# Matmuls without a reader between TensorE's ring steps, in the second half of each head of the first attention

## What is computed

```python
q, k = l2norm(q), l2norm(k)
cos = einsum('bhsd,bhtd->bhst', q, k)
g_dist = arccos(clip(cos, -1 + EPS, 1 - EPS))
attn_score = (1.0 + g_dist) ** (-3.2)
n_r, n_c = attn_score.sum(-1), attn_score.sum(-2)
k_tilde = n_r ** -1 * attn_score * n_c ** -1
probs = k_tilde / maximum(k_tilde.sum(-1), 1e-12)
out = einsum('bhst,bhtd->bhsd', probs, v)
```

## Time and profile before

| | |
|---|---|
| median of 3 runs | 3972.32 us (3971.55 to 3972.55) |
| the profiled execution's own time | 3976.55 us |
| its span, first to last instruction | 3974.8 us |
| mean granted clock of TensorE | 0.784 |
| busy: PE, DVE, ACT, POOL | 81%, 75%, 80%, 30% |
| one head of the loop | 133.12 us |

### The profile page before, as it was taken

One profiled execution on the slowest core, in us unless ns is written; L12 is line 12 of the kernel. 1 busy time (PEld: TensorE's weight loads), 2 busy tenths in 40 slices (PEclk: granted clock), 3 DMA queues, 4 the chain that ended last, 5 costly groups with the idle time before them and its releaser, 6 DMA issues. The chain is left out here.

```text
span 3974.8 us, 59836 instructions
## 1 busy us (share of the span) xinstructions
PE 3205.7 (81%) x18880; PEld 1330.2 (33%) x18880; DVE 2999.1 (75%) x4716; ACT 3186.7 (80%) x2690; POOL 1201.9 (30%) x746
## 2 busy tenths in 40 slices
PE   4777787878787878787877675888888888888899
PEld 2311121112111211121111132355555555555547
DVE  6777877887788777877788798888787787788411
ACT  2799989998999899989999665488788787888822
POOL 2201100110011001101100043377677777777700
PEclk8776566556655665666567698799999999999999
DMA  1000000000000000000000126011001100110000
GB/s 39 31 7 7 0 6 6 6 0 6 6 6 0 6 6 6 0 6 6 6 0 10 35 89 188 22 30 36 23 22 38 28 23 23 39 28 22 20 17 11
DMA packets 59566, 85.93 MB, mean 22 GB/s; under 512 B 9808, under 2 KB 45904, under 8 KB 58960
## 3 DMA queue, kind: packets, MB, share of 16 engines
q1 hardware_dynamic: 59344, 83.06, 7.2%
HBM read 52.44 MB, written 30.54 MB: 21 GB/s over the span
## 5 line engine op out<-in xcount | busy, mean ns | idle before, releaser
L1086 POOL TENSOR_TENSOR lo<-pr,hi 128x1024 f16<-128x1024 f32 x384 | 915.6, 2409 | 391.3 <-ACT hi L1212 389.2
L1135 DVE TENSOR_REDUCE mx<-mx_ps 128x1 f32<-128x512 f32 x1024 | 660.3, 684 | 170.1 <-PE mx_ps L1250 166.4
L656 PE MATMUL r_ps<-qst,kst 72*128 72x512 bf16 x1024 | 576.1, 569 | 239.3 <-DVE wt L474 143.1
L1227 ACT ACTIVATE pr<-s_ps 128x1024 f32<-128x1024 f32 x512 | 531.3, 1038 | 269.0 <-PE s_ps L1271 238.9
L660 PE MATMUL r_ps<-mst 110*128 110x512 f16 (+1 forms) x1024 | 537.0, 535 | 158.7 <-DVE wt L444 115.9
L1212 ACT ACTIVATE hi<-pr 128x1024 f16<-128x1024 f32 x512 | 546.9, 1069 | 0.0
L287 POOL COPY mono_x<-two 128x256 f32 (+1 forms) x16 | 8.5, 531 | 1716.8 <-PE m_ps L629 1663.1
L1250 PE MATMUL mx_ps<-ka,qa 128*128 128x512 f16 x1024 | 385.5, 398 | 138.2 <-DVE mx L1135 115.4
L587 ACT ACTIVATE wt<-wt 128x2048 f32<-128x2048 f32 x256 | 484.9, 1895 | 0.5
L578 ACT ACTIVATE wt<-wt,theta_bias 128x8192 f32<-128x8192 f32 (+2 forms) x96 | 462.6, 4834 | 0.2
L1290 PE MATMUL pv_ps<-vh,hi 128*128 128x129 f16 x4096 | 432.3, 222 | 11.0 <-ACT sums L1218 5.8
(11 more groups left out here) (179 smaller groups left out, 4380.9 us busy)
## 6 DMA issues: line engine op xcount, KB each, us to landing
qk<-stg SPq DMA_DIRECT2D x6, 2048.0 KB, 13.6
vh<-v SPq DMA_DIRECT2D x16, 520.0 KB, 3.7
qa<-qk SPq DMA_DIRECT2D x16, 512.0 KB, 3.9
ka<-qk SPq DMA_DIRECT2D x32, 256.0 KB, 4.7
v<-v_st SPq DMA_DIRECT2D x3, 2080.0 KB, 7.9
qst<-parts_dram SPq DMA_DIRECT2D x144, 32.0 KB
kst<-parts_dram SPq DMA_DIRECT2D x144, 32.0 KB
qk<-stg SPq DMA_DIRECT2D x4, 1024.0 KB, 8.0
```

The costliest lines, as they stand in the source:

```text
L656: mm = eng.matmul(r_ps[:, r % 2, :], kst[:, cols(k)], qst[:, cols(n_, BANK)], start=True, stop=True)
L1086: eng.tensor_tensor(lo[:, i % NHL, :, :], pr_slot(i), hi[:, i % NHL, :, :], ALU.subtract).then_inc(lo_done, 1)
L1135: eng.tensor_reduce(mx4[:, q // NCH, q % NCH:q % NCH + 1], mx_ps[:, q % 2, :], AX.X, ALU.max)\
L1227: eng.activation(pr_slot(i), s_ps[:, i % 2, :, :], ACT.Exp, scale=SM).then_inc(exp_done, 1)
```

## The change

`keep_clock(many)` issues `many` matmuls of 111 rows, 128 stationary columns and 512 moving columns into `t_ps`, from the factors in `mst`; no semaphore counts them and nothing reads what they write. In the loop behind the squares one stands ahead of each ring step, and three more behind step 89, in the cube of root tile 4. Since `finish_rows` reads `t_ps`, TensorE waits for `attn_ready` once before the first of them.

```diff
+                def keep_clock(many):
+
+                    for _ in range(many):
+                        eng.matmul(t_ps[:, :, :].rearrange("p a b -> p (a b)"), mst[0:KM, 1, cols(0)],
+                                   mst[0:KM, 0, cols(0, BANK)], start=True, stop=True)
+
...
                     for r in range(done, NRING):
+                        if r == max(done, s_at(0) + 1) and not first:
+                            eng.wait_ge(attn_ready, h)
+                        if r > s_at(0):
+                            keep_clock(1)
                         ring(h, r)
                         if r == q_at(RA - 1) + 9 and not first:
                             turn(h - 1)
                         if r == q_at(RA) + 9 and not last:
                             for j in range(4):
                                 turn_factors(h + 1, j)
+                        if RA <= r // 12 and r in [q_at(j) + 9 for j in range(RA + 1, NQ - 3)]:
+                            keep_clock(3)
                         for p in range(3):
                             if r == q_at(NQ - 3 + p) + 9:
                                 weigh(h, p)
```

## The result

Five runs of each: 3996.22 us (3989.16 to 3997.94) against 3972.32 (3971.55 to 3976.34). The ratio is 1.0055, 95% interval 1.0041 to 1.0070: slower by half a per cent, with a TensorE clock that is clearly higher.

What follows compares the result with a forecast made beforehand. It took the first attention to be tied to ScalarE, TensorE often at its low clock. Gains of 0.7 + 0.5 + 2.0 = 3.2 us, 15 times, plus 3.5 in the last head, made 51.5: 3921 us, range 3895 to 3960.

Steps and rivals of the forecast that it cites:

- The wait for attn_ready: Ahead of step 38: costs nothing, since TensorE can't do that step before 957.49 and DVE's last copy ends at 952.5.
- At 1.2 GHz TensorE is the bound: Ring steps with an extra matmul: 0.85 us against 0.695, 0.16 lost a step; at 2.4 GHz 0.43 of 0.62, nothing lost.
- Log tiles: Steps 38 to 67: clock rises after 5.6 us, 0.7 us a head gained; ends 1.24 gained, 4.8 lost.
- rival B: Log tiles' 72-row steps never lift the clock, TensorE becomes the bound: 2.3 us a head slower, 4009 us; chance 0.11.
- Root tiles 3 and 4: Any gain is hidden by DVE's 3.93 us wait for ACT, up to 3.9 lost too; pause grows, clock falls there.
- Root tiles 5 to 7 and the head's end: After the pause: 0.5 us a head gained in the tiles, 2.0 at the end from earlier, faster weighings.
- Rival A: Clock falls in each hole, at least every 10 us: about 1.2 us a head gained, 3953 us; chance 0.20.

Runs made afterwards that it cites:

- Run 1: The change without its part in the log tiles: extra matmuls only ahead of steps 68 to 127 and behind step 89; 3916.73 us, ratio 0.9852.
- run 5: The kernel before the change, with the 72-row steps padded by zeros to 128 rows and no extra matmuls; 3928.17 us, ratio 0.9884.
- run 8: The changed kernel plus 18 more extra matmuls behind the wait for attn_ready, in TensorE's idle time before the log tiles; 3898.99 us, ratio 0.9809.
- run 7: The changed kernel with its 72-row steps kept, but extra matmuls of 128 rows from a tile of zeros; 3888.78 us, ratio 0.9790.
- run 3: The changed kernel with its 72-row steps padded by 56 rows of zeros to 128; 3878.10 us, ratio 0.9753.
- run 4: The changed kernel with extra matmuls of 72 rows instead of 111 everywhere; 4070.70 us, ratio 1.0238.

## Why the prediction was wrong

The forecast was 3921 us, the range 3895 to 3960, slower at 0.11. Step by step:

- *The wait for attn_ready*: right. It ends at 1095.4, and the step behind it starts at 1100.37.
- *At 1.2 GHz TensorE is the bound, 0.85 us a step; at 2.4 GHz the extra matmul costs nothing*: right. Both were seen: 0.85 us a step in the log tiles, and four reads of DVE in 2.47 us where the clock was high.
- *Log tiles: "I take 5.6 us, the middle; ends 4.4 and 7.0"* until the clock rises. **This is the step that failed.** It took every full stretch for the same; the two that I read had been streams of squares (109 rows, with steps of 72 and 110 between) and of weighings (128 rows). With 72 and 111 rows in turns it never rose. The term was 0.7 us gained and came out 4.6 lost, next to the end that I had worked out for no rise, 4.8. That is rival B in its place and mechanism, with its mark that a stretch with 72-row steps among it rose late. I gave it 0.11 since "each full stretch seen did lift the clock". Nor was that end in my range: "1.4" a head is not the sum of the terms' lower ends, which is -4.8 - 1.0 - 0.5 = -6.3.
- *Root tiles 3 and 4*: half right. The pause did grow to 5.49 us, though nothing had been gained in the log tiles. The clock was low in it, but in the head shown it fell at 1146.9, before the pause began, after TensorE had stood idle for 2.74 us in the cube of root tile 4.
- *Root tiles 5 to 7 and the head's end, 2.5 us*: right in sum, 2.5 us less at L560. On DVE root tiles 5 to 7, from L484 behind the pause to L433, took 32.3 us before. They took 31.0 in 6 of the 13 heads and 32.7 in the 7 in which the clock fell once more, a mean gain of 0.4 where I had 0.5. Run 1, where nothing but these is left, measured 3917 us where the forecast had 3921 with the log tiles' 0.7 in it.
- *Rival A*, the clock that keeps falling: it falls in the first half of a head, as it did before; at the sigmoids; in the cube of root tile 4; and in 7 of 13 heads once more, in root tile 7, behind the cube of root tile 6. Six of those seven are the shorter ones (134.3 to 134.5 us). So this fall is not where the time went, and the case did not come by itself.

The sum of rival B, 2.3 us a head and 4009 us, was too dark by 13: a head lost 1.7, and the unchanged code behind took 8.9 us less. The Trainium skill (TensorE: Matmul & The Clock Gate, A second HAM failure mode: psum-queue depth-cycling) describes a clock that goes up and down between groups of matmuls. The changed kernel's heads do show one, but the time went where the clock stayed down. The Trainium skill (TensorE: Matmul & The Clock Gate, What's actually happening) has the clock set by how busy the engine has been of late. The 24 us at 0.50 with no idle time between matmuls differ from that: busy time is not the whole of it here.

What stays open: how exactly rows are counted, and whether they weigh in the same way on holding the clock as on lifting it (the first half of run 5's heads suggests it, no run isolates it). Nor was it tried which of the 93 extras a head are needed with padded steps.

## What to carry to other kernels

Matmuls without a reader pay only where they lift the clock, and until they do they take the place of real ones: read, for the very mix that the stage would stream, whether the granted clock rose behind it, and where the mix has few contracted rows, pad them with zeros, which cost no time here. Try the padding by itself first: without a single extra matmul it gained 1.2% (run 5). Where a mix can't lift the clock, it may still hold it across an idle time (run 8, 3899 us), but rows that let the clock rise again were worth more here (run 7, 3889, and run 3, 3878). And a higher mean clock is not a result: here it rose from 0.784 to 0.865 while the kernel became slower.

## What the runs showed of the hardware

- A stream of 512-column matmuls without a pause, alternating 72 and 111 contracted rows, left the clock at 0.50 for 24 us; with 128 and 111 rows, or 72 and 128, the wait that it caused was gone.
- Rows of zeros (run 3) and whole matmuls of zeros (run 7) were enough for the clock to rise in the log tiles.
- Steps of 110 and 111 rows with 72-row extras between them left the clock at 0.50 for 8 us, behind 24 us with 72 rows in both; it rose 3.1 us after the first of the 32 transposes of 128 rows that followed (run 4).
- The same 72 and 111 rows, at DVE's pace of 0.60 us a step, held the clock at 1.00 for 18.5 us once it was there (run 8).
- Contracting 128 rows in place of 72 did not lengthen a matmul of 512 columns: at 0.50 they start 0.43 us apart with 128 and 111 rows (run 3) as with 72 and 111 (the changed kernel).
